# Branch-prefetch hints at the top of the two engine loops of an audio tower kernel

## The chip, the cores and the metric

The kernel runs on one core of one Trainium2 chip. The metric is the device time of one execution in microseconds (us): from the start of the program on the core to its end. A core has five engines, each with a sequencer of its own that reads a stream of instructions: TensorE (PE for its matmuls, PEld for its weight loads), VectorE (DVE), ScalarE (ACT), GpSimd (POOL) and SyncE (SP, which here only issues DMAs). They meet through semaphores. A name with a q behind it (PEldq, ACTq) is the sequencer of that engine: waits, register operations, branches and hints run there.

## The reference

The input x is 64 sequences of 375 rows of 256 floats. Rows are padded to 376 and paired, which gives 188 tokens a sequence. Everything is float32.

```python
h = _L0_tok_ref(x, ...)                                # strided conv, mean of the pair, layer norm
h = h + _L0_attn_ref(_layernorm(h), ...)               # attention over the 64 sequences, 16 heads of 16
h = h + _L0_ffn_ref(_layernorm(h), ...)                # gated FFN, activations and weights in blockwise FP4
h = h + _L1_attn_ref(_layernorm(h), ...)               # causal linear attention, 16 heads of 64
h = h + _L1_ffn_ref(_layernorm(h), ...)                # layer norm, 256 -> 1024 -> 256, int weights
```

In the first layer the attention of a token position runs over the 64 sequences; in the second it runs along the 188 tokens of one sequence.

## The kernel before

The program has two stages, one after the other, with an intermediate array h2 in HBM between them.

`layer0` (lines 171 to 866) works in 94 tiles, each of 2 token positions x 64 sequences = 128 rows. Every engine has a function `slot(t, par)` with its share of the work at time t: tile t enters, tiles t-1 to t-4 are in later phases, so five tiles are in flight. `layer1` (lines 877 to 1575) works in 32 slots of 2 sequences; a slot is 8 chunks of 2 heads, and `slot(s, par)` runs `step(s, c, par)` for c = 0 to 7. Here too chunks are pipelined: in the step of chunk g, PE first projects chunk g-1 (`c2_proj`, lines 1136 to 1146, and the lines 872 to 874 of `product3`), then makes q and k of chunk g, the scores of g-2, and so on.

The order of the work on each engine is the order in which the code is written; nothing reorders it. Engines wait for each other by counts of semaphores.

Both stages have a helper `slots` that every engine calls with its own function. It writes the first few slots out (the pipeline fills), then opens a hardware loop whose body is two slots (buffers alternate, so a trip takes one even and one odd slot), and then writes the last slots out. In `layer0` the loop goes from t = 6 to 90 in steps of 2: 42 trips, line 385. In `layer1` it goes from s = 3 to 29: 13 trips, line 1058. A loop exists once in each engine's stream and closes there with an addition to the counter (ALU_OP) and a COMPARE_BRANCH, which carries the line number of the loop's head. It is taken 41 and 12 times, and falls through the last time. Each trip starts with a register operation of the same line (FUSED_REGOPS or MOVE), and then the work of slot t or s. On PE in `layer0` that is the convolution of tile t (line 439), behind the transposes of `xq` (line 421) that end the trip before. On PE in `layer1` it is `c2_proj` of the last chunk of the slot before; it waits for three semaphores:

```python
wait_g(pe, "qk_lo", g + 1, 2)
wait_g(pe, "sq_lo", g + 1)
wait_g(pe, "phi_ready", g)
```

`sq_lo` is counted up by POOL's subtraction in line 1543 (tile sqs_lo). In the last step of a slot POOL does two other operations ahead of it: line 1569 (h3, bias added) and line 1535 (yT_lo). PE's last matmuls of a slot are those of line 1246 (`fc1`).

Of the kernel before, what the change touches and what calls it, by code (L numbers as in the profile page):

```python
# [170 lines left out]
def layer0(nc, x, conv_w, conv_b, tok_g, tok_b, qkv_w, q_b, k_b, v_b, out_w, out_b, gate_w, up_w, down_w,  # L171
           h2_dram, ident, eps, exponent, w1, w1_loaded, wq, wk, wv, wo):
    with ExitStack() as ctx:
# [205 lines left out]
        def slots(eng, slot):  # L379

            first = 6
            last = first + (TILES - first) // 2 * 2 - 4
            for t in range(first):
                slot(t, t % 2)
            with eng.Fori(first, last, 2) as t:
                slot(t, 0)
                slot(t + 1, 1)
            for t in range(last, TILES + 4):
                slot(t, t % 2)

        with nc.Block() as block:
            @block.sync
            def _(sp):
                def load(t, par):
                    wait(sp, "conv_done", t - 1)
                    sp.dma_start(xT[par][:].rearrange("p c t -> p (c t)"), x[bass.ds(t * 128, 128), :])\
                        .then_inc(S[f"x_loaded{par}"], 16)

                def store(w, par):
                    wait(sp, "h2_ready", w + 1)  # L400
                    for j in range(2):
                        dst = h2_dram[:, bass.ds(2 * w + j, 1), :].rearrange("b a d -> b (a d)")
                        sp.dma_start(dst, h2[par][64 * j:64 * j + 64, :]).then_inc(S[f"h2_stored{par}"], 16)

                def slot(t, par):
                    if exists(t, -1):
                        load(t + 1, 1 - par)
                    if exists(t, 4):
                        store(t - 4, par)

                load(0, 0)
                slots(sp, slot)
                for par in range(2):
                    wait_stored(sp, "h2_stored", TILES - 2 + (TILES + par) % 2, par)

            @block.tensor
            def _(pe):
# [152 lines left out]
                pe.wait_ge(wfold, 6 + 2 * KC)  # L570
                pe.wait_ge(wcopied, len(JOBS))
                slots(pe, slot)

            @block.scalar
            def _(act):
# [87 lines left out]
                act.wait_ge(wload, 16 * 12)  # L663
                act.wait_ge(wfold, 5 + 2 * KC)
                slots(act, slot)

            @block.vector
# [209 lines left out]
def layer1(nc, omega, bo, ln_g, ln_b, fc1_q, fc1_s, fc1_b, fc2_q, fc2_s, fc2_b, h2_dram, out, ident, eps, exponent,  # L877
           w1, w1_memory, w1_loaded):
    GCH = SLOTS * CH
    with ExitStack() as ctx:  # L880
# [167 lines left out]
        def slots(eng, step):  # L1048

            last = 3 + (SLOTS - 5) // 2 * 2  # L1050

            def slot(s, par):
                for c in range(CH):
                    step(s, c, par)

            for s in range(-1, 3):
                slot(s, s % 2)
            with eng.Fori(3, last, 2) as s:
                slot(s, 1)
                slot(s + 1, 0)  # L1060
            for s in range(last, SLOTS + 3):
                slot(s, s % 2)
# [26 lines left out]
        with nc.Block() as block:  # L1089
            @block.sync  # L1090
            def _(sp):
                def step(s, c, par):
                    if c == 1 and has_slot(s + 1):
                        wait(sp, "xn_ready", s + 1, QT)
                        wait(sp, "h3_start", s + 1)
                        sp.dma_start(hx[:, 0:2, :], h2_dram[bass.ds((s + 1) * 2, 2), 0:HEAD, :].rearrange("b t d -> t b d"))\
                            .then_inc(S["h2_loaded"], 16)
                        for i in range(2):
                            sp.dma_start(hx[64 * i:64 * i + 64, 2, :],
                                         h2_dram[bass.ds((s + 1) * 2 + i, 1), OV:TOK, :].rearrange("b t d -> (b t) d"))\  # L1100
                                .then_inc(S["h2_loaded"], 16)
                    if c == 2 and has_slot(s - 3):
                        wait(sp, "out_ready", s - 2, 8)
                        r, stored = res[1 - par], S[f"out_stored{1 - par}"]
                        sp.dma_start(out[bass.ds((s - 3) * 2, 2), 0:HEAD, :].rearrange("b t d -> t b d"), r[:, 0:2, :])\
                            .then_inc(stored, 16)
                        for i in range(2):
                            sp.dma_start(out[bass.ds((s - 3) * 2 + i, 1), HEAD:TOK, :].rearrange("b t d -> (b t) d"),
                                         r[64 * i + HEAD - OV:64 * i + 64, 2, :]).then_inc(stored, 16)

                slots(sp, step)
                for par in range(2):
                    sp.wait_ge(S[f"out_stored{par}"], 48 * ((SLOTS + 1 - par) // 2))

            @block.tensor
            def _(pe):
# [157 lines left out]
                def step(s, c, par):  # L1274
# [16 lines left out]
                    run_place(table, s, c, 2, par)  # L1291

                slots(pe, step)

            @block.scalar
            def _(act):
# [72 lines left out]
                def step(s, c, par):  # L1369
# [11 lines left out]
                    place(s, c, 2, par)  # L1381

                slots(act, step)

            @block.vector
# [240 lines left out]
```

## Time and profile before

| | us |
|---|---|
| median of 3 runs | 4994.09 |
| lowest, highest | 4993.77, 5003.55 |
| profiled execution, its own time | 4997.49 |
| its span, first to last instruction | 4995.6 |
| busy: PE | 4558.8 (91%) |
| busy: DVE, ACT, POOL | 3369.4, 2485.1, 1861.2 |
| mean granted TensorE clock | 0.979 |

The span is divided as follows. Constants and weights of the first stage take until about 185 us, its tiles until about 1920 us, the weights of the second stage until about 1960 us, and the 32 slots of the second stage the rest. "Busy" leaves out the sequencers' own operations. "Idle before" is time in which an engine did nothing ahead of an instruction, put down to the semaphore that came last; "issue" there means that the engine waited for nothing that the profile shows, so its sequencer was late.

### The profile page before, as it was taken

How to read it: one execution, taken by the hardware profiler on the slowest of the kernel's cores; microseconds unless marked ns; L12 is line 12 of the kernel's file. 1: busy time of each engine (PE TensorE's matmuls, PEld its weight loads, DVE VectorE, ACT ScalarE, POOL GpSimd, SP SyncE). 2: the span in 40 equal slices, each digit the busy share in tenths (PEclk: the TensorE clock that was granted, in tenths of full speed). 3: DMA queues.
4: the chain of work that ended last, by engine and by line, in shares of the span. 5: the costliest groups of instructions: out<-in, count | busy, mean ns of one | idle time of the engine just before them, and what ended most of it. 6: DMA issues, size and time to landing. Idle time of an engine off the chain costs nothing.

```text
span 4995.6 us, 118242 instructions
## 1 busy us (share of the span) xinstructions
PE 4558.8 (91%) x42264; PEld 3897.5 (78%) x42264; DVE 3369.4 (67%) x7101; ACT 2485.1 (50%) x5312; POOL 1861.2 (37%) x2018
## 2 busy tenths in 40 slices
PE   3999999999999994899999999999999999999997
PEld 2777777777777773888888888888888888888886
DVE  4788888888888883466656656656656666666665
ACT  1555555555555552455545545445455445445453
POOL 1344444444444431233433433433433433433433
PEclk9999999999999996999999999999999999999998
DMA  2000000000000001000000000000000000000000
GB/s 79 19 20 21 22 19 22 19 22 20 21 22 19 22 16 40 5 11 8 11 11 8 11 11 8 11 11 8 11 11 8 11 11 8 11 11 8 13 6 10
DMA packets 64998, 79.89 MB, mean 16 GB/s; under 512 B 8758, under 2 KB 51126, under 8 KB 64438
## 3 DMA queue, kind: packets, MB, share of 16 engines
q1 hardware_dynamic: 64566, 74.07, 5.1%
q8 instruction: 278, 4.55, 0.4%
q14 instruction: 154, 1.26, 0.1%
HBM read 49.40 MB, written 24.64 MB: 15 GB/s over the span
## 4 chain that ended last, share of the span: by engine, by line
PE 47%; POOL 5%; issue 4%; DVE 3%; ACT 2%; ACTq 0%; POOLq 0%; DMA 0%; DVEq 0%; SPq 0%
PE bA L872 9%; PE bA L873 8%; PE bA L874 8%; PE bS L1158 3%; PE bO L1181 2%; PE bB L872 2%; PE bA L1245 2%; PE bB L873 2%; PE bB L874 2%; PE bB L1144 2%; PE bB L1145 2%; PE bA L1246 1%; POOL res L1560 1%; POOL res L1562 1%; POOL sqs_lo L1543 1%
## 5 line engine op out<-in xcount | busy, mean ns | idle before, releaser
L1543 POOL TENSOR_TENSOR sqs_lo<-sq,sqs_hi 128x768 fp32r<-128x768 f32 x256 | 476.9, 1863 | 961.0 <-ACT sqs_hi L1298 953.2
L1389 DVE TENSOR_TENSOR qk_lo<-bA,qk_hi 128x384 fp32r<-128x384 f32 x512 | 283.4, 555 | 664.1 <-ACT qk_hi L1298 661.0
L1317 ACT ACTIVATE phi<-bB 128x768 f32<-128x768 f32 x256 | 207.8, 812 | 737.2 <-PE bB L1145 737.2
L1535 POOL TENSOR_TENSOR yT_lo<-tanh_y,yT_hi 128x384 fp32r<-128x384 f32 x256 | 258.9, 1011 | 566.3 <-ACT yT_hi L1298 566.3
L1298 ACT ACTIVATE qk_hi<-bA 128x384 fp32r<-128x384 f32 x512 | 251.1, 490 | 216.3 <-PE bA L874 216.3
L1399 DVE TENSOR_TENSOR aT<-bS,mask 128x1024 f32<-128x1024 f32 x256 | 311.2, 1215 | 1.2 <-PE bS L1163 1.2
L471 PE MATMUL gu<-gate_sb,xqT 128*128 128x352 f32 x752 | 265.8, 476 | 22.3 <-DVE hh L724 20.6
L872 PE MATMUL bB<-qk_lo,omega_hi 128*128 128x384 f32 x512 | 189.4, 370 | 105.2 <-issue 83.6
L1307 ACT ACTIVATE sq<-bA 128x384 f32<-128x384 f32 x512 | 250.4, 489 | 60.4 <-DVE qk_lo L1389 58.6
L500 PE MATMUL bank<-down_sb,hqT 128*128 128x256 f32 x1128 | 279.0, 390 | 1.0 <-ACT hqT L577 1.0
L617 ACT ACTIVATE tanh_g<-gu 128x352 f32<-128x352 f32 x188 | 87.1, 463 | 379.9 <-PE gu L471 379.9
L112 POOL TENSOR_TENSOR hh<-hh,small 128x704 f32<-128x704 f32 x94 | 135.1, 1437 | 375.3 <-DVE small L106 375.3
L593 ACT ACTIVATE kblk<-gu,kb_masked,rowmask 128x128 f32<-128x128 f32 x752 | 270.8, 464 | 0.0
L500 PEld LDWEIGHTS bank<-down_sb,hqT 128*128 128x128 f32 x1128 | 207.9, 191 | 71.7 <-issue 32.6
L872 PE MATMUL bA<-fc_lo,yT_hi 128*128 128x256 f32 x768 | 230.1, 300 | 29.1 <-DVE h L1442 16.4
L471 PE MATMUL gu<-up_sb,xqT 128*128 128x352 f32 x752 | 254.7, 462 | 0.0
L1347 ACT ACTIVATE pre<-bA,fc1b,fc1s 128x384 f32<-128x384 f32 x256 | 171.4, 670 | 162.0 <-PE bA L1246 161.4
L872 PE MATMUL bA<-wo_lo,attT_hi 128*128 128x256 f32 x768 | 226.8, 295 | 20.8 <-DVE qk_lo L1389 5.3
L872 PE MATMUL bA<-wv_lo,xT_hi 128*128 128x256 f32 x768 | 229.4, 299 | 13.6 <-ACT sq L1307 1.0
L1245 PE MATMUL bA<-hT_lo,fc_w 128*128 128x384 f32 x512 | 210.4, 411 | 21.8 <-DVE h L1442 14.8
L1158 PE MATMUL bS<-phi 64*64 64x192 f32 x4096 | 225.6, 335 | 0.0
L835 POOL TENSOR_TENSOR rstd<-moments,eps 128x1 f32<-128x1 f32 x282 | 53.4, 190 | 458.5 <-DVE moments L675 458.5
(230 smaller groups left out, 14898.0 us busy)
## 6 DMA issues: line engine op xcount, KB each, us to landing
xT<-in_x SPq DMA_DIRECT2D x94, 256.0 KB, 2.6
h_scratch<-h SPq DMA_DIRECT2D x188, 64.0 KB, 1.9
hx<-h_scratch SPq DMA_DIRECT2D x32, 256.0 KB, 2.7
out<-res SPq DMA_DIRECT2D x32, 256.0 KB, 2.1
hx<-h_scratch SPq DMA_DIRECT2D x64, 64.0 KB, 2.5
out<-res SPq DMA_DIRECT2D x64, 60.0 KB, 1.9
q<-in_fc_q SPq DMA_DIRECT2D x2, 1024.0 KB, 6.3
wq_sb<-in_wq SPq DMA_DIRECT2D x1, 1024.0 KB, 4.9
```

Source lines behind the costliest of these rows:

```text
L471: last = pe.matmul(gu[:, b, 0:GW], xqT[:, c, :], w[:, c, r * GW:(r + 1) * GW], start=c == 0, stop=c == KC - 1)
L500: last = pe.matmul(cv[:, 0:DM], hqT[0:w, f, :], down_sb[0:w, f, :], start=f == 0, stop=f == len(F0C) - 1)
L593: act.activation(kblk[:, c, :, j, :], src, ACT.Identity, bias=kb_masked[:, c, j:j + 1], scale=rowmask[:, j:j + 1]).then_inc(S["qk_copied"], 1)
L872: pe.matmul(out, lhs[0], rhs[1], start=start, stop=False)
L873: pe.matmul(out, lhs[1], rhs[0], start=False, stop=False)
L874: return pe.matmul(out, lhs[0], rhs[0], start=False, stop=stop)
L1158: pe.matmul(SC[o:o + 64, h, q], phi[b][p, 1, k], phi[b][p, 0, q], start=True, stop=True)
L1245: pe.matmul(A[:, k, 0:NT], w, hT[1][:, k, :], start=True, stop=False)
L1389: dve.tensor_tensor(dst, src, hi.bitcast(fp32), ALU.subtract).then_inc(S[done], 1)
L1399: dve.tensor_tensor(aT[b][:], SC[:, :, 0:ST], mask[:].unsqueeze(1).broadcast_to([128, 2, ST]), ALU.mult)\
L1535: pool.tensor_tensor(yT[1][:, f % RING, :], tanh_y[f % 2][:], yT[0][:, f % RING, :].bitcast(fp32), ALU.subtract).then_inc(S["y_lo"], 1)
L1543: pool.tensor_tensor(sqs[1][:], sq[:], sqs[0][:].bitcast(fp32), ALU.subtract).then_inc(S["sq_lo"], 1)
```

## The change

In both `slots` helpers the loop is opened by another form of the same call. It names the engine (the loop still exists only on the engine that calls) and asks for a hint to the closing branch. For that the call emits one more instruction, BRANCH_PREFETCH_HINT, which names the closing COMPARE_BRANCH and its target, as the first instruction of every trip. It is an instruction of the sequencer. Nothing else is added, removed or moved, and the closing branch stays as it is.

```diff
@@ layer0, slots
-            with eng.Fori(first, last, 2) as t:
+            with nc.Fori(first, last, 2, engines=(eng.engine,), hint_back_edge=True) as t:
                 slot(t, 0)
                 slot(t + 1, 1)
@@ layer1, slots
-            with eng.Fori(3, last, 2) as s:
+            with nc.Fori(3, last, 2, engines=(eng.engine,), hint_back_edge=True) as s:
                 slot(s, 1)
                 slot(s + 1, 0)
```

On PE at the head of the loop of `layer0` (line 385). ISA rows are the sequencer's register operations; UNCONDITIONAL_BRANCH is the entry into the loop, so the trip begins behind it:

```order
 L421 MATMUL bank<-ident,xq 128x128 x2
 L385 UNCONDITIONAL_BRANCH
+L385 BRANCH_PREFETCH_HINT
 L385 ISA
 L437 ISA
```

One row is new, between the transposes of xq of the trip before and what precedes the convolution.

On PE at the head of the loop of `layer1` (line 1058):

```order
 L1246 MATMUL bA<-hT_hi,fc_w 128x384
 L1058 UNCONDITIONAL_BRANCH
+L1058 BRANCH_PREFETCH_HINT
 L1058 ISA
 L63 REGISTER_ALU
```

Again one row is new, between the last `fc1` matmul of a trip and the register operations and waits of `c2_proj`. DVE, ACT, POOL and SP get the same two rows at the heads of their loops.

## Rows read from the trace of the kernel before

**Rows 1.** The page: busy shares of the engines, granted clock in 40 slices.
```profile
PE 4558.8 (91%) x42264; PEld 3897.5 (78%) x42264; DVE 3369.4 (67%) x7101; ACT 2485.1 (50%) x5312; POOL 1861.2 (37%) x2018
...
PEclk9999999999999996999999999999999999999998
```
**Rows 2.** Who waited for whom: waiter, releaser, us in total, times, longest.
```profile
PE bB L872 <- issue: 83.6, 56, 4.5
...
PE bB L872 <- POOL sqs_lo L1543: 21.6, 16, 2.1
...
PE bank L439 <- issue: 7.4, 41, 0.3
```
**Rows 3.** Line 1058: count, duration ns min/median/max, first and last start us.
```profile
L1058 PEldq COMPARE_BRANCH  x13: 83/3947/4270, 2393.5 to 4628.3; - x13
L1058 ACTq COMPARE_BRANCH  x13: 40/45/45, 2393.7 to 4628.6; - x13
```
**Rows 4.** Line 385, the same view.
```profile
L385 PEldq FUSED_REGOPS  x42: 41/41/46, 185.1 to 1743.7; - x42
...
L385 PEldq COMPARE_BRANCH  x42: 83/215/249, 223.0 to 1781.5; - x42
```
**Rows 5.** DMA by queue, 2393.5 to 2580.3 us: packets, MB, share.
```profile
q8 instruction: 17, 0.28, 0.7%
q14 instruction: 10, 0.08, 0.1%
```
**Rows 6.** DMA, 250 to 1750 us: all packets, and the only queue.
```profile
DMA packets 24016, 31.08 MB, mean 21 GB/s; under 512 B 3792, under 2 KB 13904, under 8 KB 24016
...
q1 hardware_dynamic: 24016, 31.08, 7.7%
```
**Rows 7.** Timeline across a taken branch of line 1058: start, duration, [idle before].
```profile
2393.53 1.81 POOL L1543 TENSOR_TENSOR sqs_lo<-sq,sqs_hi 128x768 fp32r<-128x768 f32 x1
...
2393.69 0.33 PE L1246 MATMUL bA<-hT_hi,fc_w 128*128 128x384 f32 x1
...
2397.90 0.68 PE L872 MATMUL bB<-qk_lo,omega_hi 128*128 128x384 f32 x1 [3.88 <-issue]
```
**Rows 8.** Timeline of PE where the loop ends, branch not taken.
```profile
4628.49 0.34 PE L1246 MATMUL bA<-hT_hi,fc_w 128*128 128x384 f32 x1
4630.29 0.41 PE L872 MATMUL bB<-qk_lo,omega_hi 128*128 128x384 f32 x1 [1.46 <-POOL sqs_lo L1543]
```
**Rows 9.** Windows: stretch, length, engines' busy us (instructions), granted clock, DMA share, GB/s.
```profile
2213.80:2304.60 90.80, 86.62 (x908) 79.31 (x908) 57.31 (x123) 46.88 (x88) 35.04 (x27) 1.00 0.04 11
4539.50:4630.30 90.80, 86.89 (x909) 79.68 (x909) 57.55 (x125) 46.90 (x88) 35.02 (x27) 1.00 0.03 10
4630.30:4720.80 90.50, 86.72 (x909) 79.56 (x909) 56.97 (x124) 46.84 (x88) 35.05 (x27) 1.00 0.04 11
4720.80:4811.20 90.40, 86.64 (x909) 79.52 (x909) 57.51 (x125) 46.78 (x88) 35.01 (x27) 1.00 0.02 6
...
2397.90:2401.30 3.40, 3.40 (x11) 3.40 (x12) 0.00 (x0) 0.00 (x0) 1.94 (x2) 0.50 0.04 10
```
**Rows 10.** Timeline of PE across a taken branch of line 385.
```profile
641.10 0.41 PE L421 MATMUL bank<-ident,xq 128*128 128x128 f32 x2 [0.54 <-POOL xq L112]
641.68 1.56 PE L439 MATMUL bank<-conv_sb,xT 128*128 128x256 f32 x6 [0.17 <-issue]
```
**Rows 11.** Timeline of ACT across the same branch, and where the loop ends.
```profile
2401.58 0.81 ACT L1317 ACTIVATE phi<-bB 128x768 f32<-128x768 f32 x1 [7.24 <-PE bB L1145]
...
4632.32 0.81 ACT L1317 ACTIVATE phi<-bB 128x768 f32<-128x768 f32 x1 [3.16 <-PE bB L1145]
```

## The prediction, made before the changed kernel ran

> **What bounds the kernel now.** I read the page first. PE is busy 91% of the span and no other engine over 67% [rows 1], so what PE waits for is what counts. Next I read the list of waits, for PE alone. Its longest single entry is the first matmul of `c2_proj`, L872 into bB: 83.6 us in 56 waits, the longest 4.5 us, with no releaser at all, only "issue" [rows 2]. A wait without a semaphore points at the sequencer, so the third view is the lines of the two loops. In layer1 the closing COMPARE_BRANCH on PE has a median of 3947 ns over 13, and a minimum of 83 ns; in layer0 the same instruction takes 215 ns [rows 3, 4]. The trace has 13 of the first kind from 2393.5 to 4628.3 us, of which 12 are taken and the last falls through. So a taken branch costs PE's sequencer 3.9 us in layer1 and almost nothing in layer0.
>
> The DMA queues tell the two apart. Between two branches of layer1 17 packets run on one instruction queue and 10 on the other, 0.28 and 0.08 MB [rows 5]: code is fetched all through the trip. Over 1500 us of layer0 all 24016 packets belong to the data queue [rows 6]: the body stays where it is and nothing is fetched. So the long branch is a fetch of the loop's head. That is what a hint could take away in layer1, and in layer0 there is nothing to take.
>
> The timeline across a branch shows the price on PE: the last L1246 starts at 2393.69 and takes 0.33, L872 starts at 2397.90, 3.88 us idle [rows 7]. And a second price: in the 3.4 us behind it the granted clock is 0.50, that is 1.2 GHz of 2.4 [rows 9]. A 3.9 us idle PE comes back at the lower level, and that first matmul takes 0.68 instead of 0.41 us [rows 7, 8].
>
> **Layer1, the gain.** The idle time doesn't go to zero. `c2_proj` also needs sqs_lo, and POOL makes it from 2393.53 for 1.81 us, to 2395.34; PE was done at 2394.02 [rows 7]. So PE would wait 1.32 us for POOL at least. Where the loop ends and the branch isn't taken, this is just what the trace shows: 1.46 us, released by POOL sqs_lo [rows 8]. The gap falls from 3.88 to about 1.45, by 2.4 us a trip. What is late next is POOL's sqs_lo, with two other operations ahead of it.
>
> The clock: the slots around the 1.46 us wait ran at 1.00 [rows 9], so a gap of that size does not cost the clock. Instead of pricing matmuls at half clock I take both effects together from whole slots. The trip time with a taken branch is (4628.3 - 2393.5) / 12 = 186.2 us [rows 3]. Slots of the loop that no taken branch touches: the first one of the first trip takes 90.8, the last one of the last trip 90.8, together 181.6 at clock 1.00 [rows 9]. Difference 4.6 us, and 12 x 4.6 = 55 us. Of these 2.4 are the gap and 2.2 the clock and its echo. The written-out slots behind the loop take 90.5 + 90.4 = 180.9 [rows 9], which gives 5.3 a trip and 64 us; but they have constants in place of register operations, which the hint doesn't remove. 55 is my value, 64 the upper end. As lower end I take 4.0 a trip, 48 us, if a branch whose target is present, 0.2 us as in layer0 [rows 4], still stands on the path; I expect it hidden by the 1.3 us for POOL. The 13 hints on PE lie in the same cover; without that cover they would cost as much apiece as below.
>
> The other engines: ACT's first work of a trip is phi, which comes out of PE's `c2_proj` [rows 11]. At the loop's end it started 3.16 us after ACT's previous operation. So for that long ACT's own branch and fetch are covered even when PE is no longer late. DVE starts a trip with a subtraction that needs ACT's copy, later still. If the hint worked on PE alone, nearly the same gain would be there; if it worked on all but PE, none.
>
> A rule speaks against all this. The Trainium skill (Runtime: NRT & Kernel Launch, section "Instruction fetch mechanics") says that prefetch is purely sequential and that a taken branch to a block outside the window forces a fetch before execution goes on. On the second half the trace agrees, by the 3947 ns. Were the first half true of a hinted branch too, the gain would be nothing; that is the first rival.
>
> **Layer0, the cost.** One sequencer instruction per trip on each engine, 42 times. On PE it is bare: the transposes of xq wait 0.54 us for POOL, so the sequencer has no lead, and the convolution follows with 0.17 us idle, "issue" [rows 10], in which the branch and two register operations pass. The trace has no hint, so I bound it. Below, at zero: a gain is excluded, since that branch finds its target present [rows 6]. From above it costs what the dearest resident sequencer instruction of this line costs, 215 ns [rows 4]: 42 x 0.215 = 9 us. The nearest row is FUSED_REGOPS, 41 ns of its own [rows 4], with some 60 ns to the next one, a choice of mine that lets the two register operations fit in the gap beside the tail of the branch. I take 0.1 us: 42 x 0.1 = 4 us lost. DVE, ACT and POOL are idle more than PE [rows 1], and SP only issues DMAs; I add nothing for them. Falling through at a loop's end may now cost more, if the hinted line took the place of the next one: at most two branches of 3.9 us, 8 us, which I put only into the upper end.
>
> **Sum.** 4997.5 (the profiled execution, 1.9 above its span) - 55 + 4 = 4946.5. The profiled one lies 3.4 above the median of the runs, so against 4994.1 the forecast is 4943. Its own range: 4994 - 64 = 4930 with layer0 free, and 4994 - 48 + 9 = 4955, some 4960 with a costly exit.
>
> **The rivals.** First, the hint doesn't do what it says for a body of this size. It stands at the top, and the branch comes after 17 fetched lines [rows 5]; if the line is fetched when the hint runs, it is overwritten long before. The branch stays at 3.9 us and the 4 us of layer0 are lost: 4998, no change that a measurement can tell. For it: the sequence in the trace is that of a fetcher that runs on ahead in order. Against it: the hint names the branch as well as the target, which would be of no use to a fetch at once.
>
> Second, it helps by half: the target's fetch starts early but not early enough, and the branch takes some 2 us. Then the gap is 2.0 to 2.5 us; if the clock holds, 1.5 + 2.2 us are won, 12 x 3.7 = 44; if it falls, 12 x 1.5 = 18. That is 4954 to 4980, with 4970 in the middle.
>
> Third, on the other side: in layer0 the body of every engine is resident [rows 6]. A hint that fetches its target regardless of that may displace a line that is still needed, and a body that never missed would miss once a trip. At the price of layer1's branch that is 41 x (3.88 - 0.17) = 152 us, so 4994 + 152 - 55 = 5091. It decides from 55 / 41 = 1.3 us a trip on. Against it: the head of the loop is present, so a hint for it has nothing to fetch.
>
> **How the numbers follow.** Forecast 0.75, first rival 0.13, second 0.06, third 0.06. A measurement of this kernel tells about 0.2%, 10 us. The forecast and the second rival are faster, and the first is within 10 us, less a little chance that its cost passes that. Faster 0.81, same 0.12, slower 0.07. The range from 4928 takes in all of the forecast and the second rival, to 4982; the first and the third rival stay out, 0.19.
>
> **What would show it.** In the changed profile PE's COMPARE_BRANCH of line 1058 should have a median near 0.2 us; L872 behind it should show about 1.4 us idle, released by POOL sqs_lo, and windows across the branch a clock of 1.00; a trip 181.6 us. The instruction queues should carry about as many packets in layer1, the target's one issued ahead of the branch, and still none in layer0. A trip of layer0 should be 0.1 us longer. The prediction is wrong if the branch of line 1058 still takes over 1 us, if the clock still falls to 0.50 with a gap of 1.4 us, or if instruction packets appear between 250 and 1750 us.

## The result and the profile after

The changed kernel takes 4968.1 us (median of 5 runs, 4964.0 to 4971.3), the kernel before 4994.8 beside it: a ratio of 0.9943, 95% interval 0.9929 to 0.9958, so 21 to 36 us less. The forecast was 4943. The time lies in the stated range and on the stated side, but only half of the forecast 51 us came, and it lies outside the forecast's own range (4930 to 4955, 4960 with a costly exit). The profiled execution has a span of 4969.5 us, 26.1 below that of before.

The two loops, by line, in the profile after: count, duration in ns min/median/max, first and last start in us. These answer to [rows 3, 4].

```profile
L1058 PEldq BRANCH_PREFETCH_HINT  x13: 36/40/40, 2221.6 to 4418.9; - x13
...
L1058 PEldq COMPARE_BRANCH  x13: 88/1701/2011, 2403.2 to 4600.8; - x13
L1058 ACTq COMPARE_BRANCH  x13: 44/49/49, 2403.4 to 4601.0; - x13
...
L385 PEldq BRANCH_PREFETCH_HINT  x42: 31/31/45, 184.6 to 1749.6; - x42
...
L385 PEldq COMPARE_BRANCH  x42: 88/223/261, 222.5 to 1787.5; - x42
```

In the second loop PE's branch fell from 3947 to 1701 ns, not to 0.2 us. A trip takes (4600.8 - 2403.2) / 12 = 183.1 us, before 186.2. In the first loop the hint costs 31 ns of its own, but a trip grew from (1781.5 - 223.0) / 41 = 38.01 to (1787.5 - 222.5) / 41 = 38.17. Not all of this need be the hint's: in the twelve profiles of this case without a hint in the first loop such a trip takes 38.01 to 38.07, by the build.

Two taken branches of the second loop in the timeline of PE, and POOL at the first of them. They answer to [rows 7].

```profile
2586.87 0.34 PE L1246 MATMUL bA<-hT_hi,fc_w 128*128 128x384 f32 x1
2589.20 0.44 PE L872 MATMUL bB<-qk_lo,omega_hi 128*128 128x384 f32 x1 [1.99 <-POOL sqs_lo L1543]
...
2770.76 0.33 PE L1246 MATMUL bA<-hT_hi,fc_w 128*128 128x384 f32 x1
2773.04 0.44 PE L872 MATMUL bB<-qk_lo,omega_hi 128*128 128x384 f32 x1 [1.96 <-POOL sqs_lo L1543]
```
```profile
2586.77 1.81 POOL L1543 TENSOR_TENSOR sqs_lo<-sq,sqs_hi 128x768 fp32r<-128x768 f32 x1
```

The wait is now put down to POOL, as forecast, but the reader must look at POOL's own end: 2586.77 + 1.81 = 2588.58, and PE starts only at 2589.20. The branch, still some 2.0 us long here, ends about when POOL does, and the register operations behind it come on top. The gap is 2.0 us where 1.45 was forecast; over the twelve taken branches it is 1.58 to 1.99, 1.75 in the mean.

Windows of the profile after, with the columns of [rows 9]: the 3.4 us behind each of those two gaps, the two trips that they begin, and the slot behind the loop.

```profile
2589.20:2592.60 3.40, 3.40 (x14) 3.40 (x15) 0.17 (x1) 0.67 (x1) 3.07 (x2) 0.67 0.10 24
2773.00:2776.40 3.40, 3.36 (x19) 3.37 (x20) 0.21 (x1) 1.08 (x2) 3.04 (x2) 1.00 0.08 24
...
2589.20:2773.00 183.80, 175.34 (x1816) 160.88 (x1816) 114.94 (x247) 93.58 (x176) 70.10 (x54) 0.99 0.03 10
2773.00:2955.00 182.00, 173.70 (x1816) 159.25 (x1816) 114.62 (x246) 93.56 (x176) 70.13 (x54) 1.00 0.03 10
4602.70:4694.70 92.00, 86.72 (x908) 79.60 (x908) 57.05 (x124) 46.78 (x88) 35.07 (x27) 1.00 0.04 11
```

Gaps of 1.99 and 1.96 us look alike; behind the first, part of the 3.4 us ran at 1.2 GHz (0.67), behind the second none (1.00). The trips differ by 1.8 us. Of the 12 taken branches 8 were followed by the lower clock; before, all 12 were. The 8 trips behind a fall take 183.7 us in the mean, the 4 others 182.1.

At the end of each loop something new stands. DVE, behind the first loop, and ACT, behind the second:

```profile
1816.11 0.42 DVE L738 TENSOR_TENSOR h<-bank,h0b 128x256 f32<-128x256 f32 x1 [2.20 <-issue]
...
4646.14 0.52 ACT L1298 ACTIVATE yT_hi<-tanh_y 128x384 fp32r<-128x384 f32 x1 [1.83 <-issue]
```

Neither has a releaser. At the same instructions before there is no such wait. Here is DVE's: L738 followed L724 without a gap.

```profile
1807.39 0.52 DVE L724 TENSOR_TENSOR hh<-hh,gu 128x352 f32<-128x352 f32 x1
1807.86 0.42 DVE L738 TENSOR_TENSOR h<-bank,h0b 128x256 f32<-128x256 f32 x1
```

The books, profile against profile, by the starts of PE's branches: second loop 12 x (183.1 - 186.2) = -37.2 with the unrounded starts; first loop 41 x 0.16 = +6.5; ahead of the first of them -0.5; from the last branch of line 385 to the first of line 1058, 615.7 against 612.1, +3.6; behind the last of line 1058 +1.5, which is the slot of 92.0 against 90.5 [rows 9]. Sum -26.1, as the spans have it.

DVE's wait of 2.20 us lies in the +3.6. It stands in both profiles with a hint in the first loop and in none of the twelve others, so it is the hint's. But this stretch takes 610.9 to 614.4 us in those twelve, so how much of the wait reaches the end is not shown. ACT's wait stands in this profile alone: in `l1_only`, below, with the same hints in the second loop, ACT doesn't wait there, and the slot takes 91.1 us.

Code fetches of the profile after in the trip from 2586.9 to 2770.6, by queue:

```profile
q1 hardware_dynamic: 1708, 1.56, 2.8%
q8 instruction: 16, 0.26, 0.6%
```

Against [rows 5] queue 14 is gone: 10 packets of 8 KB a trip became none. Queue 8 went from 17 to 16. Between 250 and 1750 us there is still no instruction packet.

### The profile page after: what moved, and what is told of

It reads as the page before. It is cut to its first block, busy times and chain, and to the rows that moved or that the text cites. A ratio compares the mean times of both kernels' runs of the same rounds, so it can differ in the third digit from the quotient of the medians.

```text
span 4969.5 us, 118517 instructions
## 1 busy us (share of the span) xinstructions
PE 4546.9 (91%) x42264; PEld 3884.3 (78%) x42264; DVE 3369.4 (68%) x7101; ACT 2485.5 (50%) x5312; POOL 1865.2 (38%) x2018
## 4 chain that ended last, share of the span: by engine, by line
PE 46%; POOL 5%; issue 4%; DVE 3%; ACT 2%; ACTq 0%; POOLq 0%; DMA 0%; DVEq 0%; SPq 0%
PE bA L872 9%; PE bA L874 8%; PE bA L873 8%; PE bS L1158 3%; PE bO L1181 2%; PE bA L1245 2%; PE bB L872 2%; PE bB L1145 2%; PE bB L1144 2%; PE bB L873 2%; PE bB L874 2%; PE bA L1246 1%; POOL res L1562 1%; POOL res L1560 1%; POOL sqs_lo L1543 1%
```

## The experiments

Each run is beside runs of the kernel before on the same chip; ratios are to those, with 95% intervals. The runs come from two chips, on which the kernel before takes 4995.3 and 4999.1 to 5000.2 us, so across them the ratios are compared, not the times. "Trip" is a trip of the second loop. Of the runs below only `l0_only` has a hint in the first loop. Each has one profile; counts of trips are of that one execution.

### Where the hint's gain and cost lie

`l1_only`: the hint in the second loop alone.

```diff
-            with nc.Fori(first, last, 2, engines=(eng.engine,), hint_back_edge=True) as t:
+            with eng.Fori(first, last, 2) as t:
```

> The hint in the second loop alone (line 1058), the first loop as before. Theory: the hint of the first loop is pure cost, 0.15 us a trip x 42 = 6.3 us, and some 2 us more behind that loop's end, where an engine waits for code; so this kernel runs some 8.5 us faster than the changed one, about 4959.5, its second stage unchanged (trip 183.1 us). Rival: the 9.7 us by which the second stage starts later in the changed kernel are differences between executions; then the time is 4968 as in the changed kernel.

Measured: 4962.1 us, ratio 0.9931 (0.9914 to 0.9947), beside 0.9943 of the changed kernel. The intervals overlap. The direction is the expected one; a saving of 8.5 us is not told from none by these times.

`l0_only`: the hint in the first loop alone.

> The hint in the first loop alone (line 385); the second loop as before. Theory: nothing is fetched there, so it only costs: 0.15 us a trip on PE (19.34 for 19.19 us in the slot with the branch), 42 x 0.15 = 6.3 us, and about 2.2 us behind the end of the loop, where PE waits 1.70 instead of 0.57 us for POOL's xq: 8.5 us slower than before. Rival: a cost on PE that the rest absorbs by the end of the stage, so that under 3 us are left of it.

Measured: ratio 1.0015 (1.0006 to 1.0024), 3 to 12 us slower, median 5007.7 against 5000.2. PE's branches of line 385:

```profile
L385 PEldq COMPARE_BRANCH  x42: 80/216/269, 221.9 to 1784.0; - x42
```

A trip takes (1784.0 - 221.9) / 41 = 38.10 us, 0.09 above before, 0.07 below the changed kernel, and 0.03 above the slowest build without a hint there. So the first loop's hint is pure cost, and its size differs between the two builds. Where the rest of the 7.5 us comes from is not settled; of the 6.3 us expected of the trips the rows show 41 x 0.09 = 3.7.

`l1_pe` and `l1_not_pe`: the hint in the second loop on PE alone, and on all engines but PE.

```diff
-            with eng.Fori(3, last, 2) as s:
+            with nc.Fori(3, last, 2, engines=(eng.engine,), hint_back_edge=eng.engine == mybir.EngineType.PE) as s:
```

`l1_not_pe` has != in place of ==.

> The hint on PE alone, in the second loop alone. Theory: ACT's and DVE's branches (3 to 3.5 us) are covered, since their first work of a trip comes out of PE's c2_proj; the time is that of l1_only, 4962, within 5 us. Rival: without their hints ACT or DVE becomes late by 1 to 2 us a trip, 4975 to 4985.

> The hint on ACT, DVE, POOL and SP, not on PE, in the second loop alone. Theory: PE's own branch stays at 3.9 us with the clock at 0.50 behind it, and ACT's and DVE's short branches bring nothing: 4994. Rival: part of the gain of the changed kernel comes from them, 4985 or less.

Measured: PE alone 4955.9 us, ratio 0.9915 (0.9898 to 0.9932), no worse than with all hints. All but PE 1.0005 (0.9996 to 1.0015), no gain. PE's branch in `l1_not_pe` and in `l1_pe`, then the code fetches of one trip in `l1_pe`:

```profile
L1058 PEldq COMPARE_BRANCH  x13: 83/3892/4110, 2397.4 to 4632.7; - x13
...
L1058 PEldq COMPARE_BRANCH  x13: 88/1643/1921, 2390.6 to 4579.0; - x13
```
```profile
q8 instruction: 16, 0.26, 0.6%
q14 instruction: 10, 0.08, 0.1%
```

Without the hints of the other engines there are 10 packets a trip on queue 14 again, and it costs nothing. The whole gain is PE's. In this profile PE's branch is as long as with all hints, the gap behind it too (1.60 to 1.90 us), but only 3 of 12 are followed by the lower clock: a trip takes (4579.0 - 2390.6) / 12 = 182.4 us.

### Why PE's branch still takes 1.7 us

The DMA view, cut to short windows, shows PE's queue 8 around a branch. In the kernel before, with the branch at 2393.55, the window from 2392 to 2393.5 has the first row below, the one from 2393.9 to 2395 has no packet of that queue, and the one from 2395 to 2396 has the second:

```profile
q8 instruction: 1, 0.02, 4.9%
...
q8 instruction: 1, 0.02, 6.4%
```

In the changed kernel, with the branch at 2403.2, the window from 2402 to 2402.6 has the row below, and from 2403.4 to 2405.8 there is none:

```profile
q8 instruction: 1, 0.02, 11.4%
```

By the packets' own starts: before, one 0.9 us ahead of the branch, one 1.6 us behind it (the target), one 4.7 us behind it; now one 1.0 us ahead, and the next 2.7 us behind. The rows don't name what a packet holds. But read so, the times fit: in place of the fetch of the next line stands that of the target, 2.5 us earlier than before, and that is about what the branch got shorter by. At all 24 taken branches of the two kernels that packet takes 1.0 to 1.4 us and the branch ends 1.3 to 1.5 us after it, 2.3 to 2.8 us after its start. A start 1 us ahead is too late.

What sets that start? Theory A: the sequencer's entry into the code line that holds the branch. (The Trainium skill, Advanced Engine Details and Errata, section "ISA Cache", gives a line as 16 KB or 256 instructions; the packets of queue 8 agree, 0.26 MB / 16; those of queue 14 have 8 KB, 0.08 MB / 10.) The next four runs move PE's loop head, and with it the branch, within the line. By my count of the instructions of a trip, which no row shows, the branch stands 44 further into its line than the head: at about 140, 244 and 3 with the head at 96, 200 and 215. Where it stands unplaced is not shown.

```diff
-            with eng.Fori(3, last, 2) as s:
+            with nc.Fori(3, last, 2, engines=(eng.engine,), hint_back_edge=True,
+                         head_slot={mybir.EngineType.PE: 96} if eng.engine == mybir.EngineType.PE else None) as s:
```

(215 and 200 in place of 96 in the others; `nohint_head96` has hint_back_edge=False.)

> As l1_only, and the head of the second loop on PE is placed 96 instructions into a code line of 256, which moves the closing branch by as much within its own line. Theory A: the hinted line is asked for when the sequencer enters the line that holds the branch, some 2.4 us ahead of it, and needs 3.9 us; with the branch 96 instructions further into its line the fetch is done in time. COMPARE_BRANCH on PE falls from 1.7 to 0.2 us, the idle time before L872 to 1.45 us (POOL), no 0.50 clock behind it, a trip from 183.1 to 181.6 us: 12 x 1.5 = 18 us, about 4942. Rival B: the fetch starts a fixed time ahead of the branch, wherever that stands; then 1.7 us stay, and the time is that of l1_only, 4959.

> As l1_head96 with the head 215 instructions into its line, which by my count (about 3884 instructions a trip, 44 over 15 lines) puts the closing branch at the very start of a line. Theory A: the hint's fetch then starts hardly ahead of the branch, COMPARE_BRANCH on PE takes 3 to 3.9 us, the clock falls at every branch, a trip costs 185.5 to 186 us: 4959 + 12 x 2.7 = 4991. Rival B: as l1_only, 4959.

> The kernel before with the head of the second loop on PE placed 96 instructions into its line, no hint anywhere. Theory A: placement alone brings nothing, the branch stays at 3.9 us, 4994. Rival: the placement itself is what helps (fewer lines a trip, or the branch nearer a fetched line), then it is faster by 5 us or more.

> As l1_only with the head of the second loop on PE at instruction 200 of its line, so that the closing branch stands at about 244 of 256. Theory A (the fetch is asked for when the sequencer enters the branch's line): with 96 it started 3.1 us ahead of the branch in 9 of 12 trips and the branch still took 0.45 us; with 104 instructions more it starts over 5 us ahead in all trips, the branch takes 0.2 us in all, and no trip has a clock of 0.50: trips of 181.8 us, 4945 to 4949. Rival C: the fetch starts at most about 3 us ahead, whatever the placement; then the times of l1_head96 come back, 4951, with exceptions to 1.6 us.

Measured: 96: 4951.1 us, 0.9916 (0.9900 to 0.9933). 215: 5002.7, 1.0012 (1.0000 to 1.0023), the gain gone. No hint and 96: 1.0000 (0.9990 to 1.0010). 200: 4953.1, 0.9912 (0.9896 to 0.9929). PE's branch with 96, 215, without a hint, and with 200. There are 14 each, since PE now also enters the loop by a branch, 183 ns, which the view counts in:

```profile
L1058 PEldq COMPARE_BRANCH  x14: 88/452/1640, 2211.5 to 4580.5; - x14
```
```profile
L1058 PEldq COMPARE_BRANCH  x14: 87/3932/4170, 2212.7 to 4635.5; - x14
```
```profile
L1058 PEldq COMPARE_BRANCH  x14: 83/3990/4386, 2211.3 to 4627.4; - x14
```
```profile
L1058 PEldq COMPARE_BRANCH  x14: 88/360/383, 2208.4 to 4579.3; - x14
```

The same hint gives branches of 0.36, 0.45, 1.7 or 3.9 us by where the branch stands in its line. Its fetch starts 9 to 11 us ahead with 200 (the last packet ahead of the branch), 3.1 us ahead in 9 of 12 trips with 96 (0.7 to 1.1 us in the other three), 0.3 to 1.1 us unplaced, and 1.4 to 1.7 us behind the branch with 215. So B (a fixed time ahead) falls, and C (at most 3 us ahead). That the trigger is the entry into the line is the reading that fits all four placements; the entry itself has no row. With 215 the fetch starts when it does without any hint (1.1 to 1.7 us behind the branch, before), so this run can't tell a hint that comes too late from one that does nothing. What sets the exceptions with 96 is open, but it is not the hint: without one and with the same head the last packet starts 3.2 to 3.3 us ahead of the branch in 4 of 12 trips and 0.8 to 1.0 us in the others. Placement without a hint brings nothing.

The gain in time is smaller than the branch's, and the expected 4942 and 4945 to 4949 were missed. With 200 the idle time is still that for POOL; PE, where the loop ends and the branch falls through:

```profile
4581.24 0.41 PE L872 MATMUL bB<-qk_lo,omega_hi 128*128 128x384 f32 x1 [1.42 <-POOL sqs_lo L1544]
...
4584.96 0.48 PE L872 MATMUL bB<-qk_lo,omega_hi 128*128 128x384 f32 x1 [2.62 <-issue]
4585.24 0.52 PE L873 MATMUL bB<-qk_hi,omega_lo 128*128 128x384 f32 x1
```

A trip is (4579.3 - 2390.2) / 12 = 182.4 us, with the lower clock behind 4 of 12 branches, where none was expected; with 96 it is 182.3, with 2 of 12. That is the trip of `l1_pe`, whose branch was not placed: as long as PE waits for POOL, a branch of 0.4 us is not shown to be worth more than one of 1.6. (In the kernels with a longer loop head all lines behind it have numbers one higher.) The last two rows are the bill for the late branch: the hinted line came in place of the next one, as I read it, and the fall-through waits 2.62 us in the middle of `c2_proj` and goes on at 1.2 GHz. The slot behind the loop takes 95.0 us instead of 90.5:

```profile
4581.30:4676.30 95.00, 88.59 (x909) 81.00 (x909) 57.17 (x124) 46.84 (x88) 34.96 (x27) 0.98 0.04 10
```

### What is late next

The prediction named POOL's sqs_lo. Four runs take away what makes it late: line 1569 (1.8 us), which the code has at the end of step 6, directly ahead of the last step, moves behind sqs_lo of step 7.

```diff
-                    if c == 6 and has_slot(s + 1):
+                    if c == 7 and has_slot(s + 1):
                         wait(pool, "h2_loaded", s + 2, 48)
                         wait(pool, "res_step", s, 2)
                         pool.tensor_tensor(h3[1 - par][:], hx[:], bc(bo_bc), ALU.add).then_inc(S["h3_start"], 1)
```

> As l1_head200, and POOL's operation of line 1569 (h3 with its bias, 1.8 us) is moved from step 6 of a slot to step 7, behind sqs_lo. Theory: what PE waits for at the head of each slot is POOL's sqs_lo, late by 1.3 to 1.5 us because of that operation; then the idle time before the first L872 of a slot falls from 1.5 us to about 0.3 in the middle of a trip and to 0.5 us at its head, about 1 us x 30 slots = 30 us: 4918. Rival: another operand of c2_proj (phi, qk_lo) is as late, or the moved operation delays something else (x4 and h5 on POOL); then under 8 us are won.

> The kernel before with POOL's operation of line 1569 moved behind sqs_lo, no hint. Theory: the slot head in the middle of a trip gains 1 us, the one at the branch nothing, since there PE's 3.9 us of fetch cover POOL; with the written-out slots about 18 slot heads x 1.1 = 20 us: 4975. Rival: the gain of l1_head200_pool over l1_head200 (47 us) was all POOL's, also at the branch; then 4950.

> Second loop alone, hints on all engines as in l1_only, not placed, with POOL's operation moved. Theory: PE's branch of 1.75 us was nearly covered by the wait for POOL; now it is bare, the idle time at the head of a trip is about 1.75 us against 0.37 with the placed head, and the clock falls in some trips: 179 + 1.4 to 2.5 = 180.4 to 181.5 us a trip, 4923 to 4936 in all. Rival: something else is as late as the branch, and it lies within 5 us of l1_head200_pool, 4906.

> Second loop alone: hint on PE only, head of PE's loop at instruction 96 of its line, POOL's operation moved behind sqs_lo. Theory: trips of 179 us at a clock of 1.00, as in l1_head200_pool; the fall-through at the loop's end costs less than there, where the slot behind it took 92.4 instead of 89.0 us, since the next line is fetched in time or later than with 200: 4902 to 4906. Rival: with 96 the branch takes up to 1.6 us in 3 of 12 trips, now bare, and the clock falls there: 4906 to 4912.

Measured: `l1_head200_pool` 4906.2 us, ratio 0.9816 (0.9800 to 0.9833); `pool_only` 4965.8, 0.9930 (0.9917 to 0.9944); `l1_only_pool` 4926.3, 0.9854 (0.9839 to 0.9869); `best` 4921.5, 0.9842 (0.9829 to 0.9856). The run called best is not: the rival's case came, PE's branch was 1.4 to 1.7 us in 5 of 12 trips with the head at 96, and the time lies even above the rival's 4912. PE at a taken branch of `l1_head200_pool`, and POOL there:

```profile
2750.09 0.34 PE L1247 MATMUL bA<-hT_hi,fc_w 128*128 128x384 f32 x1
2750.77 0.44 PE L872 MATMUL bB<-qk_lo,omega_hi 128*128 128x384 f32 x1 [0.34 <-issue]
```
```profile
2748.14 1.83 POOL L1544 TENSOR_TENSOR sqs_lo<-sq,sqs_hi 128x768 fp32r<-128x768 f32 x1
2749.93 1.84 POOL L1570 TENSOR_TENSOR h<-hx,bo_bc 128x768 f32<-128x768 f32 x1
```

POOL is done at 2749.97, before PE's last matmul ends, and 0.34 us of branch and register operations are left. No branch in this run is followed by the lower clock. The trips:

```profile
L1058 PEldq COMPARE_BRANCH  x14: 88/360/382, 2213.0 to 4538.1; - x14
```

(4538.1 - 2392.0) / 12 = 178.8 us, 2392.0 being where the first taken one stands; 3.6 less than with POOL late. POOL alone brings 0.70% (I had expected 20 us, 34 came), the unplaced hint alone 0.69%, both 1.46%: no more than their sum, given the intervals. With the head at 200 the hint brings 0.88%, with POOL's move 1.84% against a sum of 1.58, which the times barely tell apart. The trips say more: 2.1 us for POOL alone, 3.8 for the hint with the head at 200, 7.4 for both, so there the two edits help each other. And here the place of the head counts: 0.9816 against 0.9854 for the unplaced hint, intervals apart. Of my 30 us for the move behind the placed head 47 came. Of the 3.6 us a trip, 1.2 are the gap at the branch (1.60 to 0.37 in the mean), 1.5 the one in the middle of a trip, which is gone, and 0.5 the four falls of the clock at 1.6 us each; I had put 1.0 for each head and nothing for the clock.

## Why the prediction was right or wrong

**The number: in the range in part by luck.** 4968 lies above the forecast's own range. It lies in the stated one because that took in the second rival, to which I gave 0.06. And a sign that I had named for being wrong came: PE's branch still takes over 1 us.

**The mechanism: right.** A long COMPARE_BRANCH on PE, a code fetch as its cause, a second price through the clock, and PE alone deciding: `l1_not_pe` and `l1_pe` show the last, `l1_head215` that without an early fetch nothing is left, and the 1.3 to 1.5 us from the end of a fetch to the end of the branch tie the two together. The Trainium skill's rule (Runtime: NRT & Kernel Launch, "Instruction fetch mechanics") that prefetch is purely sequential does not hold for a hinted branch: a packet of queue 8 ahead of it takes the place of the one behind it, and the branch gets shorter by as much.

**The mis-sized term: "12 x 4.6 = 55".** The step that failed was that PE's branch would fall to 0.2 us and so vanish behind the 1.3 us wait for POOL. It fell to 1.7 us. I had only the cases "in time" and "useless" and one between, at 2 us, to which I gave 0.06; that one happened, with its price "12 x 1.5 to 3.7": 12 x 3.1 = 37.2 was measured. The second rival was the nearest to the truth, in its branch length and in its time (4954 to 4980 stated).

The row that could have told: in the timeline before, one instruction packet starts 0.9 us ahead of the branch although the next line is not wanted there. If that is where the fetcher makes its choice, a choice 0.9 us ahead cannot hide a fetch from whose start to the end of the branch 2.4 us pass.

**"A gap of that size does not cost the clock": true of 1.46 us, not of the gaps that came.** This is where most of the missing time went. The 8 trips behind a fall take 1.6 us more than the others, 13 of the 18 us that the second loop missed; the longer gap itself (1.75 in place of 1.45 us) is 12 x 0.3 = 4. In the fourteen profiles of this case, from 2100 us to 100 us behind the last branch of line 1058, none of the 163 gaps of PE from 1.20 to 1.54 us is followed by the lower clock, but 19 of 86 from 1.54 to 1.80 and 12 of 18 from 1.80 to 2.05 are. So the branch of 1.7 us cost little by itself and much by the clock. A branch of 0.36 us would not have mended it alone: with the head at 200 the gaps are still 1.56 to 1.62 us, 4 of 12 lose the clock, and the second loop gains 12 x (186.2 - 182.4) = 46 of the 55 us.

**Layer0: "0.1 us, 42 x 0.1 = 4": near.** 6.5 us by the profile, inside the bounds of 0 to 9. The 215 ns of the upper bound is the median of that branch and not its dearest, which is 249 [rows 4]; that makes 10.

**The exits: left out of the sum, rightly kept in the bound.** DVE waits 2.2 us behind the first loop, and the slot behind the second takes 1.5 us more, on engines whose hints gained nothing. That it is the fall-through, for a line whose place the hinted one took, fits and is not shown.

**POOL next: right,** and worth about as much as the change itself (0.70% against 0.57).

## What to carry to other kernels

Before hinting a loop, look whether its body is fetched at all: a stage without instruction packets can only lose. Where it is, a hint on the engine that bounds the stage is enough, and look at where the closing branch stands in its code line: early in a line (`l1_head215`) the hint had no time, near its end (`l1_head200`) the way out of the loop paid 4.5 us. When a stall at a loop's head is gone, look at once for the wait that it had covered; here it was worth as much again.

## What the runs showed of the hardware

- A hinted fetch starts the earlier the further into its code line the branch stands: 9 to 11, 3.1, 1.0 us ahead of the branch and 1.4 to 1.7 behind it, for branches of 0.36, 0.45, 1.7 and 3.9 us. That it is asked for at the entry into that line, and replaces the fetch of the next one, is the reading that fits. The next packet behind PE's branch starts 2.3 to 3.4 us after it, before at 1.1 to 1.7, with another at 4.4 to 5.0.
- On PE a taken branch whose target is being fetched ends 1.3 to 1.5 us after the end of the packet of 16 KB, which takes 1.0 to 1.4 us itself.
- Without hints on ACT, DVE, POOL and SP 10 packets of 8 KB a trip run on queue 14; with them none, and ACT's sequencer goes on 0.21 us behind the branch instead of 2.6 to 3.9, DVE's 0.25 instead of 2.8 to 3.5. Why the body stays resident with a hint, and not without, is open.
- Idle gaps of 1.54 to 2.05 us on TensorE are sometimes followed by 1.2 GHz and sometimes not, 31 of 104 in all: 8 of 12 in the changed kernel and 3 of 12 in `l1_pe` with the same gaps. None of 163 from 1.20 to 1.54 us was, and 71 of 72 from 3.2 to 4.3 us were.
